# Attention probabilities split before they are turned, and turned by one DMA transpose a tile

## The chip, the cores and the metric

One core of a Trainium2 chip runs the whole program. The metric is device time in microseconds (us) of one execution. The engines are PE (TensorE: matmuls, and transposes by a matmul with the identity), DVE (VectorE), ACT (ScalarE), POOL (GpSimd) and SP (SyncE, which here only issues DMAs). Each takes its instructions in the order in which the program lists them; semaphores make one wait for another.

## What is computed

Two layers on 4 x 256 tokens of width 256. The change lies in the first block, a cross attention over 256 + 1601 = 1857 keys in each of 4 batches, with 16 query heads that share 4 key heads. Cut to what matters:

```
kv_in = concat(context, x)                     # 1857 rows
k = rope(rms_norm(kv_in @ Wk));  v = kv_in @ Wv          # 4 heads of 128
q = rope(rms_norm(x @ Wq))                               # 16 heads of 128
probs = softmax(q k^T * SCALE);  attn = probs v;  x = x + attn @ Wo
```

Behind it come a mixture of experts, a window attention and a feed-forward block, which the change leaves as they are.

## The kernel before

Values of full precision are kept as two bf16 halves, a high part and the rest (low part), and a product is three bf16 matmuls: high x high, high x low, low x high. A **group** is one batch and one key head: its keys K, its values V, and 8 query **tiles** of 128 queries (4 heads x 2 halves of the 256 tokens). There are 16 groups, so 128 tiles. The code unrolls groups 0 and 1, a loop of two groups a turn (even `u = 0`, odd `u = 1`), and groups 14 and 15.

A group has 8 **slots**, one for each tile. In a slot PE forms the scores of tile t (`form_scores`, 12 matmuls in 4 PSUM banks of up to 512 keys), DVE takes the maximum of each bank (`row_max`), and ACT the exponential into `prob`, in f32 (`exponent`). One slot later the probabilities are turned, since the value product needs keys on the partitions: `turn_probs` turns 15 blocks of 128 x 128 on PE into the PSUM buffers `pT_ps`, ACT copies the high half into `pT` (`probs_high`), DVE subtracts it from PSUM for the low half (`probs_low`), and `apply_values` makes 45 matmuls from `pT` and V. These steps go in four quarters j.

The rest of a slot is work of the group's neighbours, from the table `SLOTS`, in three places (ahead of, amid and behind the value products): for the next group the projections `KV` 0 to 7 and `Q` 0 and 1 and the small turns `KT` and `QT`; for this group or the one before (`-`) the turned output `AT` and the output projection `WO`. All use the PSUM buffer `aux`. POOL computes norm and rope of every projected row (`rope`), in `POOL_ORDER`; DVE the sums of squares and the low half of V (`raw_rows`).

SP's whole program in this stage is a loop over the groups of

```
sp.wait_ge(s["kp_done"], nth("KV", PAIRS - 1, n - 2))
sp.wait_ge(s["qp_done"], nth("Q", 1, n - 2))
...                                   # DMAs of wkv, kvT, wq, tab
sp.wait_ge(s["wo_done"], nth("WO", 1, n - 2))
...                                   # DMA of wo
```

so that the loads of group n + 1 follow the wait for `WO` 1 of group n - 2, which stands in slot 1 of group n - 1.

Of the kernel before, what the change touches and what calls it, by code (L numbers as in the profile page):

```python
# [6 lines left out]
BF16 = mybir.dt.bfloat16  # L7
# [3 lines left out]
ALU = mybir.AluOpType  # L11
# [4 lines left out]
P = 128  # L16
# [10 lines left out]
NB = len(BANKS)  # L27
PAIRS = (KT + 1) // 2
# [66 lines left out]
def prepare(nc, t, x):  # L95
# [295 lines left out]
SLOTS = [  # L391
    ([], [("KV", 0)], [("KV", 1)]),
    ([("AT-", 1)], [("KV", 2)], [("WO-", 1)]),
    ([], [("Q", 0)], [("KV", 3)]),
    ([], [("Q", 1)], [("KV", 4)]),
    ([("KT", 0)], [("KV", 5)], [("KV", 6)]),
    ([("AT", 0)], [("KV", 7)], [("QT", 0)]),
    ([("KT", 1)], [("WO", 0)], [("QT", 1)]),
    ([("KT", 2)], [("KT", 3)], []),
]  # L400
FIRST_GROUP = [("KV", 0), ("KV", 1), ("KV", 2), ("Q", 0), ("KV", 3), ("Q", 1), ("KV", 4), ("KV", 5), ("KV", 6),
               ("KV", 7), ("QT", 0), ("QT", 1), ("KT", 0), ("KT", 1), ("KT", 2), ("KT", 3)]
POOL_ORDER = [x for x in FIRST_GROUP if x[0] in ("KV", "Q")]
# [26 lines left out]
def attend(nc, t, x, groups=GROUPS):  # L430
# [4 lines left out]
    with Scope(nc, "att") as sc:  # L435
# [22 lines left out]
        mx = sc.sb("mx", [P, 2, NB])  # L458
        negmax = sc.sb("negmax", [P, 4])
        es = sc.sb("es", [P, 4, NB])  # L460
        rsum, rinv = sc.sb("rsum", [P, 4]), sc.sb("rinv", [P, 4])
        prob = sc.sb("prob", [P, 2, KP])
# [4 lines left out]
        windows = sc.sb("windows", [P, 2, WIN * ROW])  # L467

        scores = sc.ps("scores", [P, NB * 512])
        pT_ps = [sc.ps(f"pT{i}", [P, 4, P]) for i in range(2)]  # L470
        out_ps = sc.ps("out", [P, 2, HD])
        aux = sc.ps("aux", [P, 512])
# [4 lines left out]
                 "exp_done", "pt_done", "pt_hi", "pt_lo", "pv_done", "sum_ready", "rinv_ready", "o_done", "seg_in", "row_ready"]  # L477
# [3 lines left out]
        gathered, stored = ([sc.sem(f"{n}{i}") for i in range(2)] for n in ("gathered", "stored"))  # L481
        DONE = {"KV": "kv_done", "Q": "q_done", "KT": "kt_done", "QT": "qt_done", "AT": "at_done", "WO": "wo_done"}
# [25 lines left out]
        with nc.Block() as block:  # L508
            @block.sync
            def _(sp):  # L510
                def load_group(n, par, b, h):
                    if not isinstance(n, int) or n >= 2:

                        sp.wait_ge(s["kp_done"], nth("KV", PAIRS - 1, n - 2))
                        sp.wait_ge(s["qp_done"], nth("Q", 1, n - 2))
# [5 lines left out]
                    if isinstance(n, int) and n == 0:  # L521
                        for dst, src in ((kw, "kw_l"), (qw, "qw_l"), (ident, "ident_l")):
                            sp.dma_start(dst[:, :], t[src]).then_inc(s["const"], 16)
                        sp.dma_start(segt_i[:, :], t["segt_l"]).then_inc(s["seg_in"], 16)
# [4 lines left out]
                load_group(0, 0, 0, 0)  # L529
                load_group(1, 1, 0, 1)  # L530
                if groups > 2:
                    with sp.Fori(1, groups // 2) as p:
                        for u in range(2):
                            load_group(2 * p + u, u, p // 2, 2 * (p % 2) + u)

            @block.tensor
            def _(pe):
                before = []

                def task(kind, n, ahead, g, u):  # L540
                    gt = g + ahead
                    par = (u + ahead) % 2
                    if before:
                        bk, bn, bg = before.pop()
                        wait(pe, s[FREE[bk]], nth(bk, bn, bg))
                    before.append((kind, n, gt))
                    if kind == "KV":
# [38 lines left out]
                def form_scores(g, u, i):  # L586
# [3 lines left out]
                    for k, (lo, n) in enumerate(BANKS):  # L590
                        if i == 0:
                            pe.wait_ge(s["kt_lo"], nth("KT", k, g))
                        wait(pe, s["exp_done"], NB * (tile - 1) + k + 1)
# [5 lines left out]
                def turn_probs(tile, i, j):  # L599
                    wait(pe, s["exp_done"], NB * tile + j + 1)  # L600
                    wait(pe, s["pt_lo"], NB * tile + j - 1)
                    for m in range(quad(j)):
                        k0 = (4 * j + m) * P
                        last = nc.tensor.transpose(pT_ps[j % 2][:, m, :], prob[:, i % 2, k0:k0 + P], ident[:, :])  # L604
                    last.then_inc(s["pt_done"], 1)

                def apply_values(tile, i, j, g, par):
                    if i == 0 and j == 0:
                        pe.wait_ge(s["v_lo"], nth("KV", PAIRS - 1, g))
                    if j == 0:  # L610
                        wait(pe, s["o_done"], tile)
                    pe.wait_ge(s["pt_lo"], NB * tile + j + 1)
                    for m in range(quad(j)):
                        k = 4 * j + m
                        for a, w in ((0, 0), (0, 1), (1, 0)):
                            last = nc.tensor.matmul(out_ps[:, i % 2, :], pT[:, i % 2, a, k, :], V[:, par, k, w, :],  # L616
                                                    start=(k, a, w) == (0, 0, 0), stop=(k, a) == (KT - 1, 1))
# [3 lines left out]
                def slot(i, g, u, first, prep, last):  # L621
                    ahead, amid, behind = (tasks_of(place, prep, first, last) for place in SLOTS[i])
                    old = not (first and i == 0) and not (last and i > 0)
                    tile, oi = TILES * g + i - 1, (i - 1) % TILES
                    og, opar = (g, u) if i else (g - 1, 1 - u)
                    if old:
                        turn_probs(tile, oi, 0)
                        turn_probs(tile, oi, 1)
# [4 lines left out]
                    if old:  # L633
                        apply_values(tile, oi, 0, og, opar)
                        turn_probs(tile, oi, 2)
                        apply_values(tile, oi, 1, og, opar)
                        turn_probs(tile, oi, 3)
# [8 lines left out]
                def group(g, u, first, prep):  # L646
                    if before:

                        bk, bn, _ = before.pop()
# [1323 lines left out]
```

## Time and profile before

| | |
|---|---|
| median of 3 runs | 2138.71 us (2136.34 to 2139.88) |
| profiled execution: its own time, its span | 2130.99 us, 2129.2 us |
| attention, groups 0 to 15 | some 184 to 1376 us of the span |
| PE busy | 1805.2 us (85%) |
| DVE, ACT, POOL busy | 1453.1, 1074.8, 1080.8 us |

The profile is one execution. Times are counted from the start of its span. Matmuls are pipelined, so the time between the starts of two rows says more of PE than their durations.

### The profile page before, as it was taken

To read this page: it belongs to the slowest core of one execution; us is meant where nothing else is said; L and a number is where in the kernel's file an instruction comes from. 1 tells how busy PE (TensorE), PEld (TensorE's weight loads), DVE (VectorE), ACT (ScalarE), POOL (GpSimd) and SP (SyncE) were. 2 spreads that over 40 slices of the span, in tenths; PEclk is the share of its full clock that TensorE was granted. 3 is DMA by queue.
4 is the path that set the end of the run, shared out by engine and by line. 5 is a ranking of instruction groups with operands and counts; after the bars stand their busy time and mean duration, and the time that the engine had idled before them with its cause. 6 is when DMAs were issued, how large, how long until landed. Compare 5 with 4: busy or idle time off the path is not lost. (4 is left out here: it accounts for less than half of the span.)

```text
span 2129.2 us, 44379 instructions
## 1 busy us (share of the span) xinstructions
PE 1805.2 (85%) x14711; PEld 1352.4 (64%) x14711; DVE 1453.1 (68%) x3940; ACT 1074.8 (50%) x2650; POOL 1080.8 (51%) x1641
## 2 busy tenths in 40 slices
PE   3447999999999999999999999757888887378997
PEld 3425788777777877877877787543544444136884
DVE  7746887877778778778868877646445554456656
ACT  2414766666666666766767766520222222054443
POOL 4413786676667659657756865100345544154110
PEclk8657999999999999999999999956989998676998
DMA  6671022112202202201220203332367766420100
GB/s 264 245 306 71 2 82 82 35 50 82 82 3 82 82 3 82 82 28 57 82 83 2 82 12 101 108 140 81 108 192 215 212 203 180 139 56 9 41 15 24
DMA packets 74760, 202.58 MB, mean 95 GB/s; under 512 B 9945, under 2 KB 40770, under 8 KB 71170
## 3 DMA queue, kind: packets, MB, share of 16 engines
q1 hardware_dynamic: 61346, 163.70, 22.8%
q0 software_dynamic: 9984, 30.42, 4.4%
q10 hardware_dynamic: 3168, 5.24, 0.7%
q8 instruction: 131, 2.15, 0.4%
q14 instruction: 131, 1.07, 0.2%
HBM read 161.67 MB, written 37.66 MB: 94 GB/s over the span
## 5 line engine op out<-in xcount | busy, mean ns | idle before, releaser
L857 DVE TENSOR_TENSOR att_pT<-att_pT 128x512 bf16<-128x512 f32 (+1 forms) x512 | 321.9, 651 | 198.4 <-ACT att_pT L754 195.7
L616 PE MATMUL att_out<-att_V,att_pT 128*128 128x128 bf16 x5760 | 385.9, 219 | 10.0 <-DVE att_pT L857 8.3
L754 ACT ACTIVATE att_pT<-att_pT 128x512 bf16<-128x512 f32 (+1 forms) x512 | 278.3, 572 | 201.4 <-PE att_pT L604 201.4
L616 PEld LDWEIGHTS att_out<-att_V,att_pT 128*128 128x128 bf16 x5760 | 350.2, 98 | 36.7 <-DVE att_pT L857 19.6
L760 ACT ACTIVATE att_prob<-att_scores,att_negmax 128x512 f32<-128x512 f32 (+1 forms) x512 | 329.5, 653 | 15.8 <-DVE att_negmax L846 14.6
L595 PE MATMUL att_scores<-att_K,att_Q 128*128 128x512 bf16 (+1 forms) x1536 | 331.0, 366 | 0.0
L844 DVE TENSOR_REDUCE att_mx<-att_scores 128x1 f32<-128x512 f32 (+1 forms) x512 | 292.2, 631 | 4.6 <-PE att_scores L595 4.5
L604 PE MATMUL att_pT<-att_ident,att_prob 128*128 128x128 f32 x1920 | 278.2, 276 | 17.4 <-issue 17.4
L595 PEld LDWEIGHTS att_scores<-att_K,att_Q 128*128 128x128 bf16 x1536 | 153.0, 100 | 149.0 <-issue 11.0
L555 PE MATMUL att_aux<-att_wkv,att_kvT 128*128 128x256 bf16 x1440 | 188.1, 282 | 42.4 <-DMA att_kvT<-kv_s 21.1
L604 PEld LDWEIGHTS att_pT<-att_ident,att_prob 128*128 128x128 f32 x1920 | 211.5, 142 | 19.1 <-issue 18.2
L555 PEld LDWEIGHTS att_aux<-att_wkv,att_kvT 128*128 128x128 bf16 x1440 | 139.6, 101 | 69.8 <-DMA att_kvT<-kv_s 21.3
L695 POOL TENSOR_TENSOR att_scaled<-att_kvraw,att_kw 128x256 f32<-128x256 f32 x120 | 82.9, 691 | 192.8 <-ACT att_kvraw L735 192.8
L1235 POOL DMA_INDIRECT y_s<-moe_ysb,moe_result_row x80 | 79.2, 990 | 156.8 <-ACT moe_ysb L1343 155.5
L697 POOL TENSOR_TENSOR att_cosd<-att_scaled,att_tab 128x256 f32<-128x256 f32 (+2 forms) x150 | 123.4, 823 | 11.8
L1333 ACT ACTIVATE moe_silu<-moe_up 128x176 f32<-128x176 f32 x96 | 30.4, 317 | 183.8 <-PE moe_up L1291 137.0
L1230 POOL DMA_INDIRECT moe_xg<-xrow_s,moe_token_row x80 | 77.6, 970 | 86.8 <-DVE moe_token_row L1400 62.2
L1291 PE MATMUL moe_up<-moe_wa,moe_xT 128*128 128x352 f32 x320 | 121.1, 506 | 0.0
L709 POOL TENSOR_TENSOR att_rs<-att_rs,att_nhalf 128x2 f32<-128x2 f32 (+2 forms) x150 | 119.4, 796 | 0.0
L735 ACT ACTIVATE att_kvraw<-att_aux 128x512 f32<-128x512 f32 (+1 forms) x128 | 73.1, 571 | 83.9 <-PE att_aux L555 83.3
L1418 DVE COPY moe_hT<-moe_ht 128x256 f32<-128x256 f32 x96 | 40.6, 423 | 100.3 <-PE moe_ht L1298 100.1
L760 ACT ACTIVATION_READ_ACCUMULATOR att_prob<-att_scores,att_negmax 128x1 f32 x512 | 108.8, 212 | 0.0
(299 smaller groups left out, 3286.2 us busy)
## 6 DMA issues: line engine op xcount, KB each, us to landing
moe_wa<-in_wa_l SPq DMA_DIRECT2D x80, 480.0 KB
att_kvT<-kv_s SPq DMA_DIRECT2D x16, 1920.0 KB
att_tab<-tab_s SPq DMA_DIRECT2D x16, 960.0 KB
att_wq<-wq_s SPq DMA_DIRECT2D x16, 512.0 KB
att_wo<-wo_s SPq DMA_DIRECT2D x16, 512.0 KB
kv_s<-prep_kvhl SPq DMA_DIRECT2D x4, 1920.0 KB
prep_kv<-in_ctx_l SPq DMA_DIRECT2D x4, 1664.0 KB, 7.6
moe_y<-y_s SPq DMA_DIRECT2D x8, 768.0 KB, 4.6
```

What stands on the lines that cost most here:

```text
L555: last = nc.tensor.matmul(o, kvT[:, par, a, c, k0:k0 + P], wkv[:, par, w, c, :], start=(c, a, w) == (0, 0, 0), stop=(c, a) == (DC - 1, 1))
L595: last = nc.tensor.matmul(scores[:, lo:lo + n], Q[:, u, a, i, :], K[:, u, w, lo:lo + n], start=(a, w) == (0, 0), stop=a == 1)
L604: last = nc.tensor.transpose(pT_ps[j % 2][:, m, :], prob[:, i % 2, k0:k0 + P], ident[:, :])
L616: last = nc.tensor.matmul(out_ps[:, i % 2, :], pT[:, i % 2, a, k, :], V[:, par, k, w, :], start=(k, a, w) == (0, 0, 0), stop=(k, a) == (KT ...
L695: eng.tensor_tensor(a, raw[:, 0:m, :], weight[:, :].unsqueeze(1).to_broadcast([P, m, HD]), ALU.mult).then_inc(linked, 1)
L697: eng.tensor_tensor(b.rearrange("p m (e f) -> p m e f", e=2), a.rearrange("p m (e f) -> p m e f", e=2), cos.unsqueeze(2).to_broadcast([P, ...
L709: eng.tensor_tensor(scale, scale, nhalf[:, 0:m], ALU.pow).then_inc(linked, 1)
L754: nc.scalar.activation(pT[:, i % 2, 0, 4 * j:4 * j + m, :], pT_ps[j % 2][:, 0:m, :], ACT.Copy).then_inc(s["pt_hi"], 1)
L760: nc.scalar.activation(prob[:, i % 2, lo:lo + n], scores[:, lo:lo + n], ACT.Exp, bias=negmax[:, i % 4:i % 4 + 1], scale=1.0, accum_out=es[ ...
L844: nc.vector.reduce_max(mx[:, i % 2, k:k + 1], scores[:, lo:lo + n], AX.X).then_inc(s["bank_max"], 1)
L857: nc.vector.tensor_tensor(pT[:, i % 2, 1, 4 * j:4 * j + m, :], pT_ps[j % 2][:, 0:m, :], pT[:, i % 2, 0, 4 * j:4 * j + m, :], ALU.subtract) ...
L1291: last = nc.tensor.matmul(up_ps[j % 2][:, 0:GU], rows, w[:, c * GU:(c + 1) * GU], start=c == 0, stop=c == DC - 1)
```

## The change

- The probabilities are split while queries are still on the partitions. ACT copies `prob` into the high half of the new tile `phl` (bf16), DVE subtracts it from `prob`; both in two **spans** of up to 1024 keys (`SPANS`), not four banks. The maxima and exponentials go by spans too.
- PE's turns are gone. SP issues one `dma_start_transpose` a tile, of both halves of `phl` (128 x 3840, bf16) into `pT`, when DVE has done the low half. This is one slot after the scores.
- The value products follow two slots behind the scores, the scaled output three.
- The PSUM banks set free become a second buffer for the tasks (`aux0`, `aux1`) and one bank for each output.
- `SLOTS` is written anew: `Q` 0 and 1 in slot 0, then `KV` 0 to 7, and POOL works in that order.
- SP's program is now written in slots, with the loads between the transposes.
- `windows`, used at the end of the stage, is laid over `tab`.

The diff, cut to its core:

```diff
 SLOTS = [
-    ([], [("KV", 0)], [("KV", 1)]),
...
+    ([], [("Q", 0)], [("Q", 1)]),
+    ([], [("KV", 0)], [("KV", 1)]),
...
+                def turn(tile, i):
+                    sp.wait_ge(s["p_lo"], NS * (tile + 1))
+                    sp.sem_inc(s["turning"], 1)
+                    sp.dma_start_transpose(pT[:, i % 2, :, :, :].rearrange("p a k q -> p (a k) q"),
+                                           phl[:, i % 2, :, :].rearrange("p a k -> p (a k)")).then_inc(turned[i % 2], 16)
+
+                def slot(i, g, u, first, prep, last):
+                    if not (first and i == 0) and not (last and i > 0):
+                        turn(TILES * g + i - 1, (i - 1) % TILES)
+                    if i == 0 and prep and not first:
+                        load_first(*batch_head(g, u, 1))
+                    if i == 4 and prep and not first:
+                        n, par, _, h = batch_head(g, u, 1)
+                        load_wo(n, par, h)
...
                 def apply_values(tile, i, j, g, par):
-                    pe.wait_ge(s["pt_lo"], NB * tile + j + 1)
+                        wait(pe, s["o_done"], tile - 1)
+                        pe.wait_ge(turned[i % 2], 16 * (TILES // 2 * g + i // 2 + 1))
...
+                def probs_high(tile, i, g, k):
+                    lo, n = SPANS[k]
+                    act.wait_ge(s["exp_done"], NS * tile + k + 1)
+                    if k == 0:
+                        wait(act, turned[i % 2], 16 * (TILES // 2 * g + i // 2))
+                    nc.scalar.activation(phl[:, i % 2, 0, lo:lo + n], prob[:, i % 2, lo:lo + n], ACT.Copy).then_inc(s["p_hi"], 1)
...
+                def probs_low(tile, i, g, k):
+                    lo, n = SPANS[k]
+                    dve.wait_ge(s["p_hi"], NS * tile + k + 1)
...
+                    nc.vector.tensor_tensor(phl[:, i % 2, 1, lo:lo + n], prob[:, i % 2, lo:lo + n], phl[:, i % 2, 0, lo:lo + n],
+                                            ALU.subtract).then_inc(s["p_lo"], 1)
```

`load_first` holds the waits for `kp_done` and `qp_done` and the DMAs of wkv, kvT, wq and tab; `load_wo` the wait for `wo_done` and the DMA of wo; `batch_head(g, u, 1)` names the group after g.

**PE, slot 0 of group 1** (a slot with the first tasks for group 2). L595/L625 are the scores, L604 the turns, L616/L638 the value products, L555 a `KV` projection, L592 a `Q` projection. Before:

```order
L604 MATMUL att_pT<-att_ident,att_prob 128x128 x8
L595 MATMUL att_scores<-att_K,att_Q 128x512 x9
L595 MATMUL att_scores<-att_K,att_Q 128x321 x3
L616 MATMUL att_out<-att_V,att_pT 128x128 x12
L604 MATMUL att_pT<-att_ident,att_prob 128x128 x4
L616 MATMUL att_out<-att_V,att_pT 128x128 x12
L604 MATMUL att_pT<-att_ident,att_prob 128x128 x3
L555 MATMUL att_aux<-att_wkv,att_kvT 128x256 x12
L616 MATMUL att_out<-att_V,att_pT 128x128 x21
L555 MATMUL att_aux<-att_wkv,att_kvT 128x256 x12
```

Now, up to the scores of slot 1:

```order
L625 MATMUL att_scores<-att_K,att_Q 128x512 x9
L625 MATMUL att_scores<-att_K,att_Q 128x321 x3
L638 MATMUL att_out<-att_V,att_pT 128x128 x24
L592 MATMUL att_aux<-att_wq,att_kvT 128x512 x6
L638 MATMUL att_out<-att_V,att_pT 128x128 x21
L592 MATMUL att_aux<-att_wq,att_kvT 128x512 x6
L625 MATMUL att_scores<-att_K,att_Q 128x512 x9
```

The turns are gone, and the first task that reads the next group's wq and kvT is a `Q` in the middle of slot 0.

**SP, group 1 and the last of group 0.** The eight transposes are those of slots 1 to 7 of group 0 and of slot 0 of group 1. Before, after the loads at the start of the stage, SP's loop over the groups began at once, with nothing between the loads:

```order
L518 DMA att_wkv<-wkv_s 128x1024
L518 ISA
L518 DMA att_kvT<-kv_s 128x7680
L519 ISA
L519 DMA att_wq<-wq_s 128x2048
L520 ISA
L520 DMA att_tab<-tab_s 128x1920
L527 DMA att_wo<-wo_s 128x2048
```

Now:

```order
L541 DMA_TRANSPOSE att_pT<-att_phl 128x30x128 x8
L522 DMA att_wkv<-wkv_s 128x1024
L522 DMA att_kvT<-kv_s 128x7680
L523 DMA att_wq<-wq_s 128x2048
L524 DMA att_tab<-tab_s 128x1920
L541 DMA_TRANSPOSE att_pT<-att_phl 128x30x128 x4
L529 DMA att_wo<-wo_s 128x2048
L541 DMA_TRANSPOSE att_pT<-att_phl 128x30x128 x3
```

The loads for group 2 stand behind the transpose of slot 0 of group 1, in the same queue.

## Rows read from the trace of the kernel before

**Rows 1.** The page: busy time (share of the span) x instructions.

```profile
PE 1805.2 (85%) x14711; PEld 1352.4 (64%) x14711; DVE 1453.1 (68%) x3940; ACT 1074.8 (50%) x2650; POOL 1080.8 (51%) x1641
```

**Rows 2.** By stretch: length, PE, PEld, DVE, ACT, POOL, clock, DMA, GB/s.

```profile
230.00:1400.00 1170.00, 1103.91 (x11209) 892.02 (x11206) 899.43 (x2311) 772.50 (x1989) 753.90 (x1320) 0.98 0.18 65
```

**Rows 3.** Waits from 400 to 1300 us: total us, times, longest.

```profile
PE att_out L616 <- DVE att_pT L857: 3.4, 11, 0.3
```

**Rows 4.** PE in order of time, one slot and the next scores: start, us.

```profile
201.42 2.52 PE L595 MATMUL att_scores<-att_K,att_Q 128*128 128x512 bf16 x12
203.77 0.83 PE L616 MATMUL att_out<-att_V,att_pT 128*128 128x128 bf16 x12
204.44 0.61 PE L604 MATMUL att_pT<-att_ident,att_prob 128*128 128x128 f32 x4
...
207.18 1.34 PE L616 MATMUL att_out<-att_V,att_pT 128*128 128x128 bf16 x21
208.36 1.47 PE L555 MATMUL att_aux<-att_wkv,att_kvT 128*128 128x256 bf16 x12
209.67 1.04 PE L604 MATMUL att_pT<-att_ident,att_prob 128*128 128x128 f32 x8
210.54 2.52 PE L595 MATMUL att_scores<-att_K,att_Q 128*128 128x512 bf16 x12
```

**Rows 5.** SP's queue in order of time, two rounds of loads.

```profile
346.10 0.33 SPq L527 DMA_DIRECT2D att_wo<-wo_s  x1
347.18 0.33 SPq L518 DMA_DIRECT2D att_wkv<-wkv_s  x1
...
419.18 0.33 SPq L527 DMA_DIRECT2D att_wo<-wo_s  x1
```

**Rows 6.** By stretch, while a group's loads run; the last number is GB/s.

```profile
348.00:354.00 6.00, 6.00 (x69) 4.70 (x67) 5.57 (x15) 3.68 (x11) 5.84 (x13) 1.00 0.95 329
354.00:358.00 4.00, 4.00 (x30) 2.79 (x29) 1.69 (x4) 2.73 (x8) 3.76 (x7) 1.00 1.00 417
```

**Rows 7.** DMA issues: KB each, median us from issue to landing.

```profile
all_x<-in_x_l SPq DMA_DIRECT2D x1, 1024.0 KB, 5.1
...
out<-all_x SPq DMA_DIRECT2D x8, 128.0 KB, 1.7
```

**Rows 8.** SP's DMA queue: packets, MB, share of 16 engines' span.

```profile
q1 hardware_dynamic: 61346, 163.70, 22.8%
```

**Rows 9.** Order in time, one slot: scores, maxima, the first low half after.

```profile
704.53 2.52 PE L595 MATMUL att_scores<-att_K,att_Q 128*128 128x512 bf16 x12
...
706.40 2.28 DVE L844 TENSOR_REDUCE att_mx<-att_scores 128x1 f32<-128x512 f32 x4
...
709.10 0.69 DVE L857 TENSOR_TENSOR att_pT<-att_pT 128x512 bf16<-128x512 f32 x1
```

**Rows 10.** DVE by shape: busy us, mean ns; last row from 500 us on.

```profile
L342 DVE TENSOR_TENSOR prep_kvhl<-prep_kv,prep_kvhl 128x1920 bf16<-128x1920 f32 x4 | 19.9, 4965 | 2.3 <-ACT prep_kvhl L253 2.3
...
L697 DVE TENSOR_TENSOR att_cosd<-att_scaled,att_tab 128x256 f32<-128x256 f32 x7 | 3.0, 425 | 0.2
...
L695 DVE TENSOR_TENSOR att_scaled<-att_qraw,att_qw 128x512 f32<-128x512 f32 x2 | 1.4, 689 | 0.0
...
L832 DVE TENSOR_TENSOR att_V<-att_kvraw,att_V 128x256 bf16<-128x256 f32 x54 | 31.7, 588 | 0.0
```

**Rows 11.** PE in order of time, around the loop's end.

```profile
476.47 1.97 PE L604 MATMUL att_pT<-att_ident,att_prob 128*128 128x128 f32 x8 [3.48 <-issue]
478.23 4.53 PE L595 MATMUL att_scores<-att_K,att_Q 128*128 128x512 bf16 x12
```

**Rows 12.** PE in order of time, scores of two slots of group 15.

```profile
1303.70 2.52 PE L595 MATMUL att_scores<-att_K,att_Q 128*128 128x512 bf16 x12
...
1311.31 2.52 PE L595 MATMUL att_scores<-att_K,att_Q 128*128 128x512 bf16 x12
```

**Rows 13.** PE in order of time, one of five small turns of the first group.

```profile
178.05 1.12 PE L567 MATMUL att_aux<-att_ident,att_kp 128*128 128x128 f32 x4 [1.41 <-DVE att_K L819]
```

More of the change, by code:

```diff
@@ L27 @@
 NB = len(BANKS)
+SPANS = [(k, min(1024, NK - k)) for k in range(0, NK, 1024)]
+NS = len(SPANS)
 PAIRS = (KT + 1) // 2
@@ L622, in slot @@
                     ahead, amid, behind = (tasks_of(place, prep, first, last) for place in SLOTS[i])
[L623 to L628, printed above, removed]
+                    old = not (first and i < 2) and not (last and i > 1)
+                    tile, oi = TILES * g + i - 2, (i - 2) % TILES
+                    og, opar = (g, u) if i >= 2 else (g - 1, 1 - u)
                     if not last:
@@ L654, in tail @@
                 def tail(g):
[L655 to L657 removed]
+                    before[:] = [(bk, bn, g - 1) for bk, bn, _ in before]
+                    for i in range(TAIL):
                         slot(i, g, 0, False, False, True)
@@ L770, in slot @@
                     tile, oi = TILES * g + i, (i - 1) % TILES
-                    old = not (first and i == 0) and not (last and i > 0)
-                    if old:
-                        probs_high(tile - 1, oi, 0)
-                        probs_high(tile - 1, oi, 1)
-                    if not (first and i < 2) and not (last and i > 1):
-                        output(tile - 2, (i - 2) % TILES)
+                    if not (first and i < 3) and not (last and i > 2):
+                        output(tile - 3, (i - 3) % TILES)
+                    if not (first and i == 0) and not (last and i > 0):
+                        for k in range(NS):
+                            probs_high(tile - 1, oi, g if i else g - 1, k)
                     for kind, n in projected(i, prep):
@@ L862, in slot @@
                     tile, oi = TILES * g + i, (i - 1) % TILES
-                    old = not (first and i == 0) and not (last and i > 0)
-                    if old:
-                        probs_low(tile - 1, oi, 0)
-                        probs_low(tile - 1, oi, 1)
                     if not last:
@@ L870, in slot @@
                         task(*x_, g, u)
-                    if old:
+                    if not (first and i == 0) and not (last and i > 0):
                         row_sum(tile - 1, oi)
-                        probs_low(tile - 1, oi, 2)
-                        probs_low(tile - 1, oi, 3)
+                        for k in range(NS):
+                            probs_low(tile - 1, oi, g if i else g - 1, k)
                     for kind, n in projected(i, prep):
```

151 lines of the change are left out of this document (69 added, 82 removed).

## Prediction

> **What bounds the kernel now.** I read the page first: PE is busy for 85% of the span [rows 1]. The table by stage then shows where: from 230 to 1400 us, the attention, PE is busy for 1103.91 of 1170 us at a granted clock of 0.98, DVE for 899.43 [rows 2]. The list of waits from 400 to 1300 us shows no long wait of PE: for the low halves of the probabilities it waits 3.4 us in all [rows 3]. So the attention is PE's own work, end to end. The order in time of one slot gives its parts, start to start: scores 203.77 - 201.42 = 2.35 us; value products 0.67 us for 12, so 0.67 + 0.67 + 1.18 = 2.5 us for 45; turns 0.87 us for 8, so 1.65 us for 15 [rows 4]. SP issues the loads of a group once in 419.18 - 346.10 = 73.1 us [rows 5]: eight slots of 9.14 us. What is left for projections and small turns is 9.14 - 2.35 - 2.5 - 1.65 = 2.6 us a slot.
>
> **What it removes.** The 15 turns on PE: 9.14 - 1.65 = 7.5 us of PE work a slot. If nothing else moved, 15 groups x 8 x 1.65 = 198 us, and some 13 us in the last group, were gained. DVE has 899.43 / 128 = 7.0 us of work a slot (the window holds all 128 tiles but a few) [rows 2], so it could follow.
>
> **What it adds: one DMA transpose a tile.** It moves 2 x 1920 x 128 x 2 bytes = 983 KB from SBUF to SBUF. The trace has no such operation. From below: the plain loads of a group run at 329 GB/s over 6 us and at 417 over the next 4, 364 in the mean [rows 6]; at 365 GB/s it is 2.7 us, and a small transfer (128 KB) lands after 1.7 us [rows 7]. That gives L = 4.4 us from issue to landing; a plain load of 1024 KB landed in 5.1 us [rows 7], in line with it. From above: the destination is written in rows of 256 bytes, 3840 of them, 240 for each of 16 engines. SP's queue moved 61346 packets in 22.8% of 16 engines' span, 0.127 us a packet [rows 8]; if each row cost a mean packet, L = 30 us. I take L = 6.5 us, near the lower end, since in bytes and engines it is most like the plain load, with half as much again for the short rows.
> The Trainium skill (DMA: Bandwidth & Descriptors, section Latency and other measured facts) gives 261 GB/s for a transpose DMA in one kernel. With that, an estimate, L = 3.8 + 1.7 = 5.5 us, and the sum below would come to 2330 us. No row here shows a transpose, so the sum goes by the bounds.
>
> **The chain that L lies on.** Call the start of a slot's scores S. Scores end at S + 2.35; the second of the two maxima takes 833 columns after that, about 0.95 us (2.28 us for 1857 columns in four pieces [rows 9]); maximum, sum and reciprocal bring the first low half to S + 3.8 (before it began 4.57 us after the scores at 704.53, after four reductions that ended late [rows 9]). The low halves are two subtractions, 1857 columns, now with both operands in SBUF. From below: in the first group, where POOL does little, two operands in SBUF cost DVE 0.425 us for 256 columns and 0.689 for 512, so 1.03 ns a column and 2.1 us for the two. From above: beside POOL's long subtractions of the preparation 1920 columns took 4.965 us, so 4.8 us. Between: the value rows' subtraction of 256 columns takes 0.588 us in the attention, 1.4 times 0.425; so 2.9 us [rows 10]. The tile is ready to turn at S + 6.9 with 0.2 us for the hand-over. Its value products stand one slot on, at 2.35 us into it. They start at S + 6.9 + L, and behind them in PE's order stand 2.5 + 2.6 us before the scores two slots after S. Two slots take 12.0 + L, one 6.0 + L/2: with L = 6.5, 9.25 us, with L = 4.4, 8.2 us. PE's 7.5 us are not reached unless L is 3 us. DVE and ACT have room in 9.25 us. So the 1.65 us come back as a wait for the transpose.
>
> **The loads move behind the turns, and next to their use.** Before, SP issued the loads for a group's preparation after the output projection in slot 1, and the first projection that reads them stood in slot 0 of the next group, six slots on; two rounds of loads are 73 us apart [rows 5]. Now SP's program is in slots. In slot 0 of a group it first waits for the low halves of the last tile (S + 6.9), issues that transpose, and then wkv, kvT, wq and tab of the next group; and PE's first projection of the next group, Q 0, stands in the middle of that same slot 0, at S + 2.35 + 1.25 = S + 3.6. Nothing hides this: behind Q 0 in PE's order stand the other value products, Q 1 and the scores of tile 1; ACT and DVE run dry, and POOL waits for raw rows. wq is landed after the transpose has left the engines (L - 1.7) and 2.75 MB (256 + 1920 + 512 KB) are through, 7.5 us at 365 GB/s, and 1.7 us more: S + 6.9 + (L - 1.7) + 9.2. Then follow Q 0 (1.3), the other half of the value products (1.25) and Q 1 (1.3). Slot 0 lasts 6.9 + (L - 1.7) + 9.2 + 3.85 = 18.25 + L: 24.75 us, some 17 of them PE standing still. These are 14 loads, in groups 1 to 14.
> After 3.48 us of idle at the loop's end PE ran at half clock: 8 turns took 1.97 us (1.04 before), 12 matmuls of the scores 4.53 us (2.52) [rows 4, 11], 0.93 + 2.01 = 2.9 us in all. I charge 2.9 us once a stall. The loop's end itself stays.
>
> **The group.** From the start of slot 1: its own 7.5 us (no wait, slot 0 was long), then three pairs of slots: 7.5 + 3 x (12.0 + L) = 43.5 + 3L. With slot 0 and the clock: 64.65 + 4L. With L = 6.5: 90.65 us against 73.1, +17.55. Times 14: **+246 us**.
>
> **Small terms.** Groups 0 and 15 have no load to wait for. Group 0: 9.25 instead of 9.14 a slot, +1. In group 15 (slots of 1311.31 - 1303.70 = 7.6 us [rows 12]) POOL is idle: 6.0 + L + 2.5 + 0.6 for two slots, 7.8 us, +2. The first group's small turns get two PSUM buffers instead of one: five waits of about 1.4 us [rows 13] shrink, -5. The last tile gets a transpose in its chain, +4. Fewer, longer instructions on ACT and DVE (8 fewer a tile) lie beside PE: 0. The value buffers, output two slots later, and windows laid over tab cost nothing while POOL's gather ends in group 15. Together +2.
> Sum: 2130.99 (the profiled execution) + 248 = 2379. The median of the runs shown is 7.7 us above the profiled one, so **2387 us**.
>
> **The rivals.**
> *The transpose is slow.* SP's queue works one after the other; with L of 12 us and more it is the bound in every slot. For: the short rows. Against: 16 engines with full rows ran at 417 GB/s [rows 6]. L = 12: 14 x (64.65 + 48 - 73.1) = +554, 2693 us. 0.22.
> *DVE's subtraction is the worse half.* With 4.8 instead of 2.9 us the chain grows by 1.9 in slot 0 and in each pair, 7.6 x 14 = +106: 2492 us. POOL is busy for 753.90 of 1170 us, with short instructions [rows 2], which speaks for less. 0.12.
> *The transpose is as fast as a plain copy.* L = 4.4: 64.65 + 17.6 = 82.25, +128: 2268 us. 0.13. The Trainium skill (Advanced Engine Details and Errata, section X-Bar Transpose) has transposes at the rate of regular DMAs on trn2, which would be this case; no row here can show it.
> *Not slower.* The loads come early enough after all: this decides from the point where they are issued 9.2 us before S + 3.6, so in the slot before. Against it is SP's order: its wait for the low halves of the tile before can't end until DVE has done the maxima of slot 0, which need PE's scores of slot 0. Even a transpose that costs nothing leaves slot 0 at 6.9 + 9.2 + 3.85 = 19.95, and with the clock and 7 slots of 7.5 us 75.35 us a group, +2.25, 31 us in all: with 26 us won in groups 0 and 15 and 5 at the start, 2139 us, no change. Were the loads hidden too, 2139 - 198 - 13 - 5 = 1923 us. Together 0.06.
>
> **How the numbers follow.** Forecast 2387 us, chance 0.47, its own range 2320 to 2450 (L from 5.4 to 7.7). Leaving out most of the slow transposes and of the last rival: 2250 to 2620. What is within 0.2% can't be told from no change. Faster 0.04 (a part of the last rival), same 0.03, slower 0.93.
>
> **What would show it.** In the profile after: PE in slot 0 waits for DMA wq some 15 to 20 us, 14 times; value products wait for the DMA of pT about 1.5 to 2 us a slot; the granted clock falls to a half after each long wait; L of the transposes is 5 to 8 us; subtractions from prob take about 1.5 us each. What would make it wrong: L far from 6.5 us (4 x 14 = 56 us for each us), transposes and loads that share the engines otherwise than one after the other, or a clock that stays low through the slots.

## The result, and the profile after

| | before | after |
|---|---|---|
| median | 2139.3 us (4 runs) | 2480.31 us (4 runs, 2473.93 to 2529.39) |
| profiled execution: own time, span | 2130.99, 2129.2 us | 2478.94, 2477.1 us |
| ratio | | 1.1553, 95% interval 1.1441 to 1.1666 (a disturbed run, 2529.39, left out) |
| a group, first scores to first scores, mean of groups 1 to 14 | 74.9 us | 97.5 us |

The change costs 341 us. From the page of after, the busy times, and SP's DMA queue:

```profile
PE 1679.5 (68%) x12661; PEld 1207.2 (49%) x12791; DVE 1466.4 (59%) x3428; ACT 990.8 (40%) x1882; POOL 1229.3 (50%) x1641
...
q1 hardware_dynamic: 556962, 289.54, 47.2%
```

PE's busy time fell by 126 us and its share by 17 points [rows 1] (130 of its matmul records are missing: PEld has 12791). POOL, whose instructions are the same 1641 as before, is busy 148 us longer; I come back to that. By stretch, after, with columns as in [rows 2]:

```profile
230.00:1400.00 1170.00, 781.54 (x7259) 589.69 (x7353) 717.76 (x1435) 544.93 (x984) 730.41 (x1075) 0.85 0.55 125
```

No engine is busy for more than 67% of the stage: it is bound by waits. These are PE's largest, 500 to 1300 us (eight groups; total us, times, longest). Before, its wait for the turned low halves was 3.4 us from 400 to 1300 us [rows 3]:

```profile
PE att_aux L592 <- DMA att_wq<-wq_s: 124.8, 8, 17.0
...
PE att_out L638 <- DMA att_pT<-att_phl: 87.3, 41, 4.3
...
PE att_scores L625 <- issue: 24.8, 5, 6.8
```

Slot 0 of a group and the next slots on PE, in order of time, as in [rows 4]:

```profile
541.22 3.58 PE L625 MATMUL att_scores<-att_K,att_Q 128*128 128x512 bf16 x11 [6.83 <-issue]
...
544.64 1.50 PE L638 MATMUL att_out<-att_V,att_pT 128*128 128x128 bf16 x24
...
563.13 2.74 PE L592 MATMUL att_aux<-att_wq,att_kvT 128*128 128x512 bf16 x6 [16.98 <-DMA att_wq<-wq_s]
565.66 2.31 PE L638 MATMUL att_out<-att_V,att_pT 128*128 128x128 bf16 x21
...
569.11 2.52 PE L625 MATMUL att_scores<-att_K,att_Q 128*128 128x512 bf16 x12
...
581.97 2.74 PE L638 MATMUL att_out<-att_V,att_pT 128*128 128x128 bf16 x24 [2.86 <-DMA att_pT<-att_phl]
```

SP's queue in slot 0, and below it all transposes (duration on SP, then issue to landing, min/median/max):

```profile
548.71 4.48 SPq L541 DMA_TRANSPOSE att_pT<-att_phl  x1
553.70 0.35 SPq L522 DMA_DIRECT2D att_wkv<-wkv_s  x1
...
554.80 0.33 SPq L523 DMA_DIRECT2D att_wq<-wq_s  x1
```

```profile
L541 SPq DMA_TRANSPOSE att_pT<-att_phl x128: 4399/4504/10693, 190.3 to 1705.4; - x128
...
DMA to landing us min/median/max: 6.3/6.4/12.8
```

Here is the stall: PE is through the first half of the value products at about 546 us and stands still until 563; wkv is issued at 553.70, wq at 554.80.

### The profile page after: what moved, and what is told of

It reads as the page before. It is cut to its first block and busy times, and to the rows that moved or that the text cites. A ratio compares the mean times of both kernels' runs of the same rounds, so it can differ in the third digit from the quotient of the medians.

```text
span 2477.1 us, 38974 instructions
## 1 busy us (share of the span) xinstructions
PE 1679.5 (68%) x12661; PEld 1207.2 (49%) x12791; DVE 1466.4 (59%) x3428; ACT 990.8 (40%) x1882; POOL 1229.3 (50%) x1641
## 5 line engine op out<-in xcount | busy, mean ns | idle before, releaser
L638 PE MATMUL att_out<-att_V,att_pT 128*128 128x128 bf16 x5760 | 422.3, 238 | 205.6 <-DMA att_pT<-att_phl 205.6
L858 DVE TENSOR_REDUCE att_mx<-att_scores 128x1 f32<-128x1024 f32 (+1 forms) x256 | 276.7, 1119 | 466.0 <-PE att_scores L625 466.0
L638 PEld LDWEIGHTS att_out<-att_V,att_pT 128*128 128x128 bf16 x5760 | 392.6, 108 | 248.1 <-issue 121.7
L625 PE MATMUL att_scores<-att_K,att_Q 128*128 128x512 bf16 (+1 forms) x1423 | 315.5, 373 | 37.5 <-issue 32.0
L873 DVE TENSOR_TENSOR att_phl<-att_prob,att_phl 128x1024 bf16<-128x1024 f32 (+1 forms) x256 | 335.4, 1350 | 3.2 <-issue 1.3
L781 ACT ACTIVATE att_prob<-att_scores,att_negmax 128x1024 f32<-128x1024 f32 (+1 forms) x256 | 262.6, 1031 | 157.5 <-DVE att_negmax L860 157.5
L625 PEld LDWEIGHTS att_scores<-att_K,att_Q 128*128 128x128 bf16 x1536 | 154.7, 101 | 191.3 <-issue 54.4
L709 POOL TENSOR_TENSOR att_scaled<-att_qraw,att_qw 128x512 f32<-128x512 f32 x30 | 39.0, 1299 | 410.5 <-ACT att_qraw L756 410.5
L774 ACT ACTIVATE att_phl<-att_prob 128x1024 bf16<-128x1024 f32 (+1 forms) x256 | 236.4, 978 | 0.0
L592 PE MATMUL att_aux<-att_wq,att_kvT 128*128 128x512 bf16 x177 | 64.3, 519 | 240.0 <-DMA att_wq<-wq_s 238.0
L711 POOL TENSOR_TENSOR att_cosd<-att_scaled,att_tab 128x256 f32<-128x256 f32 (+2 forms) x150 | 154.6, 1031 | 11.8
L592 PEld LDWEIGHTS att_aux<-att_wq,att_kvT 128*128 128x128 bf16 x192 | 22.0, 125 | 268.3 <-DMA att_wq<-wq_s 209.6
L842 DVE SCALAR_TENSOR_TENSOR att_kjunk<-att_kvraw 128x128 bf16<-128x128 f32 x240 | 118.8, 527 | 0.0
```

Source lines behind the costliest of these rows:

```text
L625: last = nc.tensor.matmul(scores[:, lo:lo + n], Q[:, u, a, i, :], K[:, u, w, lo:lo + n], start=(a, w) == (0, 0), stop=a == 1)
L638: last = nc.tensor.matmul(out_ps[i % 2][:, 0:HD], pT[:, i % 2, a, k, :], V[:, par, k, w, :], start=(k, a, w) == (0, 0, 0), stop=(k, a) == ...
L709: eng.tensor_tensor(a, raw[:, 0:m, :], weight[:, :].unsqueeze(1).to_broadcast([P, m, HD]), ALU.mult).then_inc(linked, 1)
L711: eng.tensor_tensor(b.rearrange("p m (e f) -> p m e f", e=2), a.rearrange("p m (e f) -> p m e f", e=2), cos.unsqueeze(2).to_broadcast([P, ...
L774: nc.scalar.activation(phl[:, i % 2, 0, lo:lo + n], prob[:, i % 2, lo:lo + n], ACT.Copy).then_inc(s["p_hi"], 1)
L781: nc.scalar.activation(prob[:, i % 2, lo:lo + n], scores[:, lo:lo + n], ACT.Exp, bias=negmax[:, i % 4:i % 4 + 1], scale=1.0, accum_out=es[ ...
```

## The experiments

Each kernel differs from after (or the one named) by the edit shown. In the same series of runs as an experiment the kernel before took 2122.82 to 2135.74 us; ratios are to it.

**Loads early.** SP loads two groups ahead, in slot 0, so a group's data is there a group before its use.

```diff
-                    if i == 0 and prep and not first:
-                        load_first(*batch_head(g, u, 1))
+                    if i == 0 and not last and not (isinstance(g, int) and g + 2 >= groups):
+                        load_first(*batch_head(g, u, 2))
```

> The changed kernel, but the loads of wkv, kvT, wq and tab for group g + 2 are issued in slot 0 of group g (before: for group g + 1, so next to their use). Theory (a wait of 17 us for wq and 2.9 us at half clock in each of 14 groups; the rest of the loss is the transpose in the chain): slot 0 falls to about 10 us, a group from 97.8 to about 83 us, the kernel to 2300 us (2250 to 2350); the wait of PE for wq is gone, the wait for pT stays or grows, because the 4.2 MB stand before the next transpose. Rival (the chain of scores, maxima, low halves and transpose is so slow that the wait in slot 0 only covers it): above 2420 us.

Measured 2265.72 us, ratio 1.0655 (1.0618 to 1.0692). The late loads cost 215 us. A group is now 83.2 us. PE's wait for pT grew, as expected, from 205.6 to 280.1 us over the whole span.

**Loads late, in the kernel before.** The other way round: before gets one more wait ahead of its loads.

```diff
                         sp.wait_ge(s["qp_done"], nth("Q", 1, n - 2))
+                        sp.wait_ge(s["pt_lo"], NB * (TILES * (n - 1) - 1) + NB)
```

> The kernel before with one wait more: SP issues the loads for group g + 1 only when the last low half of group g - 1 is done, which is in slot 0 of group g, where their first projection stands. No other part of the change. Theory: kvT is waited for in the middle of slot 0, some 10 us, and 2.9 us at half clock behind it, 14 times: +185 us, 2325 us (2290 to 2360). Rival (the loads are through before PE comes to them): 2139 us.

Measured 2301.72 us, ratio 1.0826 (1.0783 to 1.0868), 86.8 us a group. The loads alone, placed where the change puts them, make the old kernel slower. PE's wait, 500 to 1300 us:

```profile
PE att_aux L556 <- DMA att_kvT<-kv_s: 87.5, 9, 10.1
```

**No transposes, with late and with early loads.**

```diff
-                    sp.dma_start_transpose(pT[:, i % 2, :, :, :].rearrange("p a k q -> p (a k) q"),
-                                           phl[:, i % 2, :, :].rearrange("p a k -> p (a k)")).then_inc(turned[i % 2], 16)
...
-                        pe.wait_ge(turned[i % 2], 16 * (TILES // 2 * g + i // 2 + 1))
```

> The changed kernel without its transposes: pT is set to zero once at the start, SP still waits for the low halves before it issues the loads, and the value products read zeros (that part of the computation is left out). Theory: no wait for pT; slots 1 to 7 go at 7.7 us, the wait for wq shrinks by the 4.5 us of one transpose to 12 or 13 us; a group takes 78 us and the kernel about 2220 us (2180 to 2260). Rival (DVE and POOL, which share SBUF, hold the slots up and not the transpose): slots of 9 us and more, above 2330 us.

> Both of the edits before: no transposes (zeros in pT) and loads two groups ahead. Theory: what PE's own work gives, 7.6 us a slot, 61 us a group and the loop's ends; 1985 us (1940 to 2030). Rival (DVE or POOL is the bound behind the transposes): 8.5 us a slot or more, above 2080 us.

Measured 2345.33 us, ratio 1.1026 (1.0983 to 1.107), and 2147.25 us, ratio 1.0105 (1.0082 to 1.0127). Both times the rival's number came. The transposes cost 135 us with late loads and 118 with early ones, far from the 260 and 281 that the theory gives (2480 - 2220 and 2266 - 1985); and a kernel with no turns on PE, no transposes and no load to wait for is no faster than before, 76.8 us a group against 74.9. (What follows the last scores takes 765 us here and 771 before, so the other data behind it hardly count.) So a third cost hides behind the first two. In this trace, with transposes gone and loads early, the stage and three of its waits, 500 to 1300 us:

```profile
230.00:1400.00 1170.00, 941.84 (x9356) 706.16 (x9353) 883.37 (x1807) 679.88 (x1243) 906.44 (x1324) 0.93 0.17 60
```

```profile
DVE att_K L829 <- ACT att_K L757: 88.7, 23, 6.7
...
PE att_aux L603 <- DVE att_Q L829: 61.6, 10, 6.5
...
ACT att_kvraw L751 <- POOL att_kp L731: 40.6, 10, 4.1
```

POOL is busy for 906 of 1170 us, against 754 [rows 2]. The order in time beside one pair of DVE's subtractions shows why:

```profile
761.38 0.45 POOL L712 TENSOR_TENSOR att_sind<-att_scaled,att_tab 128x128 f32<-128x128 f32 x1
...
761.82 2.44 DVE L867 TENSOR_TENSOR att_phl<-att_prob,att_phl 128x1024 bf16<-128x1024 f32 x2
761.94 1.44 POOL L718 TENSOR_TENSOR att_cosd<-att_cosd,att_sind 128x128 f32<-128x128 f32 x1
763.34 1.49 POOL L721 TENSOR_TENSOR att_rs<-att_rs,att_nhalf 128x2 f32<-128x2 f32 x1
...
768.52 0.46 POOL L718 TENSOR_TENSOR att_cosd<-att_cosd,att_sind 128x128 f32<-128x128 f32 x1
768.93 0.71 POOL L721 TENSOR_TENSOR att_rs<-att_rs,att_nhalf 128x2 f32<-128x2 f32 x1
```

The same two steps take 1.44 and 1.49 us beside the subtraction and 0.46 and 0.71 without it: 1.8 us more in this slot. Over the stage it is some 1.3 us a slot (906 - 754 us in 122 slots). POOL falls behind, ACT's next copy of raw rows waits for POOL's key, and what stands behind that copy in ACT's, DVE's and PE's orders waits too. That was an argument until the next two runs.

**A maximum in the subtraction's place** (from the kernel without transposes and with early loads).

```diff
-                    nc.vector.tensor_tensor(phl[:, i % 2, 1, lo:lo + n], prob[:, i % 2, lo:lo + n], phl[:, i % 2, 0, lo:lo + n],
-                                            ALU.subtract).then_inc(s["p_lo"], 1)
+                    nc.vector.tensor_reduce(spare[:, i % 2, k:k + 1], prob[:, i % 2, lo:lo + n], AX.X, ALU.max).then_inc(s["p_lo"], 1)
```

> The kernel of the changed program without transposes and with early loads (2147.25 us), in which DVE, in place of subtracting the high half from the probabilities (two operands read from SBUF, one written there), takes a maximum over them (one operand, nothing but one column written). It leaves out the turned probabilities and the low halves. Theory: the subtraction keeps POOL off the SBUF while it runs, POOL's steps take 906 us of the window 230 to 1400 instead of 754, and POOL's late keys hold up ACT, DVE and PE in turn. Then POOL's steps fall back to about 0.5 us for 128x128, POOL has 10 us a group less to do, and the time is 1995, within 1950 to 2050. Rival: it is the length of DVE's own work, or the order of the waits, whatever POOL does: the maxima take about as long as the subtractions (1.1 to 1.35 us each), and the time stays within 2110 to 2160.

Measured 2003.45 us, ratio 0.9333 (0.9238 to 0.9429): 144 us less, 67.2 us a group. POOL's steps in groups, 500 to 1300 us, with the maxima and, below, with the subtractions:

```profile
L719 POOL TENSOR_TENSOR att_cosd<-att_cosd,att_sind 128x128 f32<-128x128 f32 (+2 forms) x103 | 53.7, 522 | 0.0
L712 POOL TENSOR_TENSOR att_sind<-att_scaled,att_tab 128x128 f32<-128x128 f32 (+1 forms) x102 | 52.2, 512 | 0.0
```

```profile
L711 POOL TENSOR_TENSOR att_sind<-att_scaled,att_tab 128x128 f32<-128x128 f32 (+2 forms) x103 | 80.4, 781 | 0.0
L718 POOL TENSOR_TENSOR att_cosd<-att_cosd,att_sind 128x128 f32<-128x128 f32 (+1 forms) x104 | 73.5, 707 | 0.0
```

**The same, with DVE as long as before.** One more maximum over 400 columns a slot.

> As the kernel with maxima in place of the subtraction (2003.45 us), with one more maximum over 400 columns a slot, so that DVE is busy there for as long as the subtractions took (2.7 us a slot, not 2.2). The same parts are left out. It tells the two things apart that the maximum changed at once. Theory, POOL held off the SBUF: DVE's own length costs little, and the time is 2015, within 2000 to 2045. Rival, DVE's length: 0.45 us a slot of DVE gave the gain, and the time goes most of the way back, above 2090.

Measured 2013.54 us, ratio 0.9472 (0.9419 to 0.9524). DVE's length gives 10 us back, or 30 by the ratios (1.3 us a group), not 144. Most of what the subtraction costs is its hold on POOL, not its own time.

**Half a transpose** (from loads early).

```diff
-                    sp.dma_start_transpose(pT[:, i % 2, :, :, :].rearrange("p a k q -> p (a k) q"),
-                                           phl[:, i % 2, :, :].rearrange("p a k -> p (a k)")).then_inc(turned[i % 2], 16)
+                    sp.dma_start_transpose(pT[:, i % 2, 0, :, :], phl[:, i % 2, 0, :]).then_inc(turned[i % 2], 16)
```

> The changed kernel with early loads (2265.72 us), in which the transpose takes the high half alone, so half the bytes; the low half in the turned tile is a constant zero, which leaves the low halves out of the value products' values but not their matmuls. The transpose should occupy SP 2.2 us and land after some 4.2 us instead of 4.4 and 6.4. Theory, a chain of score, split, transpose and value product in each pair of slots with POOL's work beside it: removing the transposes gave 118 us for 6.4 us each, so 2.2 us give 40, and the time is 2225, within 2200 to 2245. Rival A, the working of the prediction (every pair of slots is 12.0 us and the transpose): 2.2 us less in 4 pairs of 15 groups gives 132, 2135. Rival B, the transpose's fixed part is what counts: within 2255 to 2275.

Measured 2172.84 us, ratio 1.0147 (1.0053 to 1.0241): 93 us less, between the theory's 40 and rival A's 132, and neither's number. The transposes:

```profile
L541 SPq DMA_TRANSPOSE att_pT<-att_phl x128: 1306/1596/8371, 193.7 to 1398.3; - x128
...
DMA to landing us min/median/max: 4.1/4.1/11.3
```

Half the bytes land 2.3 us sooner, so the rate is 492 KB / 2.3 us = 214 GB/s, and 1.8 us are fixed. A group takes 77.0 us, as with no transposes at all (76.8): both theories took the cost as a straight line, and it has a knee. At 6.4 us the chain of the pair sets the slots; at 4.1 us something else sets the group. That it is POOL is argued from the equal length alone: the long slots lie elsewhere in the group than without transposes, and PE still waits 140.2 us for pT. The rest of the 118 us lies in the last group (51.2 us from its first to its last scores against 37.7) and behind it.

**The split in its own slot, loads together and spread** (from loads early). ACT's and DVE's steps for tile t move from slot t + 1 to slot t, and the transpose with them; value products stay at t + 2. SP now also waits for the value products of tile t - 2 before it issues the transpose of tile t. In the second kernel the loads go out in slots 0 to 3, kvT in two halves.

```diff
                         exponent(tile, i, 1)
+                        for k in range(NS):
+                            probs_high(tile, i, g, k)
```

> The changed kernel with early loads (2265.72 us), in which ACT makes the high half and DVE the low half in the slot of their own scores, behind the exponentials, and SP issues the transpose there; the value products stay two slots behind. Theory: the chain in a pair of slots is gone, since a transpose now has a whole slot more; what is left is POOL's work and the chain of keys, as without transposes (2147 us), plus what the transposes take of the memory ports: 2165, within 2140 to 2200. Rival: the split in its own slot makes DVE wait for ACT's exponentials and high half within the slot, with the maxima of the next scores queued behind; each slot is then 9 to 11 us, and the time is above 2230.

> As the kernel before it (the split in its own slot), and the loads of a group, which SP issued together in slot 0, are spread over slots 0 to 3. Theory: the five loads in one slot hold back the transpose behind them in slot 1, which then costs some 5 us a group; spread, they cost nothing, and the time is 60 us lower than that of the kernel before it. Rival: the transpose has a slot to spare, so that the loads cost nothing either way: within 10 us of it.

Measured 2277.91 us, ratio 1.0655 (1.0579 to 1.0731), and 2213.27 us, ratio 1.0344 (1.026 to 1.0428). The theory of the first failed: 2165 was expected. The rival's number came, but not by its mechanism, slots of 9 to 11 us: slots 1, 2 and 4 of a group take 6.6 to 7.5 us, slot 3 takes 16 to 19, slots 6 and 7 11 to 16. The second kernel says what a large part of it was: the loads in one slot delay the transposes behind them, and spreading them gives 65 us (60 expected), with 9.3 to 9.8 us for slot 3. PE waits for pT 49.4 us over the whole span then, against 135.9 in the first kernel and 280.1 with loads early.

**Exponentials left in PSUM** (from the last one). A version that computes everything, and frees POOL: DVE's subtraction reads one operand from PSUM. ACT makes the high half of a span right behind its exponential.

```diff
-                        wait(pe, s["exp_done"], NS * (tile - 1) + k // 2 + 1)
+                        wait(pe, s["p_lo"], NS * (tile - 1) + k // 2 + 1)
...
-                    nc.scalar.activation(prob[:, i % 2, lo:lo + n], scores[:, lo:lo + n], ACT.Exp, bias=negmax[:, i % 4:i % 4 + 1],
+                    nc.scalar.activation(scores[:, lo:lo + n], scores[:, lo:lo + n], ACT.Exp, bias=negmax[:, i % 4:i % 4 + 1],
...
-                    nc.vector.tensor_tensor(phl[:, i % 2, 1, lo:lo + n], prob[:, i % 2, lo:lo + n], phl[:, i % 2, 0, lo:lo + n],
+                    nc.vector.tensor_tensor(phl[:, i % 2, 1, lo:lo + n], scores[:, lo:lo + n], phl[:, i % 2, 0, lo:lo + n],
```

> A version that computes all of the output. The split in its own slot and the spread loads (2213.27 us), and ACT writes the exponentials over the scores in PSUM, so that DVE's subtraction reads one operand from PSUM and one from SBUF, as before the change. PE's scores of the next tile then wait for the low half of the same span. Theory: POOL's steps are back at 0.5 us, as with the maxima; a slot is DVE's chain of two maxima, an exponential, a high half and two subtractions, with the second exponential beside it, 7.6 to 8.5 us, and a group 66 to 70 us against 74.9 before the change: 2050, within 2000 to 2120. Rival A: the banks held until the low half put the slot at 9.5 us or more: above 2180. Rival B: it is the transposes' traffic on the memory that slows POOL and DVE, not the subtraction: POOL's steps stay at 0.6 to 0.8 us, and the time above 2150.

Measured 2225.2 us, ratio 1.0478 (1.0407 to 1.0548). The theory was right on POOL and wrong on the time. POOL's steps are back:

```profile
L734 POOL TENSOR_TENSOR att_cosd<-att_cosd,att_sind 128x128 f32<-128x128 f32 (+1 forms) x100 | 51.3, 513 | 0.0
```

It is rival A's number, with slots of 8.7 to 9.0 us in the even stretch (slots 1 to 5) rather than 9.5, and 12 to 16 in slots 6 and 7. The banks are held longer than they need be: DVE's sum of the exponentials stands ahead of the subtractions and waits for the second exponential, and the low half and the next scores wait behind it:

```profile
DVE att_rsum L876 <- ACT att_scores L795: 144.5, 70, 3.4
PEld att_scores L639 <- DVE att_phl L885: 82.9, 50, 2.3
PE att_scores L639 <- DVE att_phl L885: 76.6, 50, 2.5
```

**The sum behind the subtractions, and a levelled table** (each from the one before).

```diff
-                        row_sum(tile, i)
                         for k in range(NS):
                             probs_low(tile, i, g, k)
+                        row_sum(tile, i)
```

```diff
-    ([], [("KV", 3)], [("KV", 4)]),
-    ([], [("WO-", 1)], [("KV", 5)]),
-    ([], [("KV", 6)], [("KV", 7), ("KT", 0)]),
-    ([], [("QT", 0), ("KT", 1)], [("AT", 0), ("QT", 1)]),
+    ([], [("KV", 3)], [("WO-", 1), ("QT", 0)]),
+    ([], [("KV", 4)], [("QT", 1), ("KT", 0)]),
+    ([], [("KV", 5)], [("KV", 6)]),
+    ([], [("KT", 1)], [("KV", 7), ("AT", 0)]),
```

> The kernel with exponentials in PSUM (2225.2 us), with DVE's sum of the exponentials behind its two subtractions instead of ahead of them. All of the output is computed. There DVE waits 2 us a slot for both exponentials (144.5 us in the window 500 to 1300) before the first subtraction, which ACT's high half would have let it start 1.3 us earlier. Theory, the low half of the first span sets the next scores and so the slot: 1 to 1.3 us a slot in most slots, 2080, within 2040 to 2130. Rival: the second span ends last (DVE's second subtraction waits for ACT's second high half), the bank of the third quarter of the scores comes free as late as before, and the time stays above 2195.

> As the kernel before it, and the table of tasks is levelled: QT 0 in slot 3, QT 1 and KT 0 in slot 4, one task fewer in slot 5, KT 1, KV 7 and AT 0 in slot 6, where slots 5 and 6 held three and four. Theory: slots 6 and 7 of a group take 12 us each, since PE's third and fourth task wait for aux, which ACT and DVE empty at the end of their slot (PE waits for DVE att_Q and att_K 8 us a group); with three at most, and their inputs long ready, 5 to 6 us a group go: 75 us below the kernel before it, within 40 to 110. Rival: any third task waits as long, and three slots have one now as before: within 25 us of it.

Measured 2151.03 us, ratio 1.0105 (1.0037 to 1.0172), and 2158.3 us, ratio 1.0141 (1.0078 to 1.0204). The moved sum gives 74 us, half of what was expected; slots 1 to 4 are 7.6 to 8.2 us, but slots 6 and 7, with four and three tasks, still 11 to 13, and slot 7 16 at the loop's end. The levelled table gives nothing, which is its rival's number: slots 5 and 6 are up to 2 us shorter, slots 3 and 4 1.1 to 1.6 us longer. 2151 us is the best that I found with DMA transposes, 1% above the kernel before.

## Why the prediction was right, and where it was wrong

The forecast was 2387 us, range 2250 to 2620; measured 2480 us, in the range, slower as forecast. Of the two mechanisms that it names, the late loads are the largest cost, and the wait for the transposes is there; but a third cost, which it does not have, is larger than the second. The pieces of the 341 us, each from a pair of runs and in this order of undoing: late loads 215 (2480 - 2266), transposes 118 (2266 - 2147), POOL held up by the subtraction 144 (2147 - 2003), and against them 136 us (2139 - 2003) by which the kernel that is left, without turns and without low halves, is faster than before. In another order the pieces can be others. The kernel before itself lay between 2123 and 2139 us from series to series; measured from it in each series the pieces are 202, 118, 153 and 132, so each holds to about 15 us.

In the same parts the prediction has 233 us for the late loads ((90.65 - 8 x 9.25) x 14), 231 for the transposes (what is left of 2387 - 1923), nothing for POOL and 216 gained. The transposes are 113 us too dear and the loads 18, the gain is 80 too large, and 144 us are missing. These errors partly cancel: it is partly luck that the total is nearer than its parts. The mechanism held where the sum works it out, in the slots with a wait for wq or for a transpose; it did not hold for the kernel without them.

- **L = 6.5 us**: 6.4 measured, 4.6 us for the bytes and 1.8 fixed, where 4.8 and 1.7 were taken. It was neither the plain copy's rate (the rival at 4.4 us) nor a row at the price of a mean packet (30 us): the queue moved 495,616 packets more than [rows 8], 3872 for each transpose and so about one a row, yet each transpose was through in 4.5 us. That 6.5 was hit is luck in part: the "half as much again" for short rows had no row behind it, and each us of L is 56 us of the sum. The Trainium skill (DMA: Bandwidth & Descriptors, Latency and other measured facts) has 261 GB/s for one kernel; this trace has 214. Its statement that transposes run at the rate of regular DMAs (Advanced Engine Details and Errata, X-Bar Transpose) doesn't hold here: [rows 6] has 417 GB/s for plain loads, and the stretch with a transpose alone has 218, its DMA share full:

```profile
551.00:553.00 2.00, 0.00 (x0) 0.00 (x0) 0.00 (x0) 0.00 (x0) 0.00 (x0) 0.50 1.16 218
```

- **Slot 0**: 24.75 us and 2.9 for the clock, 27.65; measured 25.6 to 29.1. PE's wait for wq, said to be 15 to 20 us, was 16.98 in the slot shown and 15.6 in the mean (124.8 in 8). The order was right, the reason for the later issue partly not: it isn't that loads queue on the DMA engines behind the transpose, SP itself is held 4.48 us by it and issues wkv at 553.70. The experiments with loads early and with loads late in the kernel before confirm the step by 215 and 175 us, where the sum has 233.
- **Three pairs of 12.0 + L = 18.5 us**: in group 13 they took 19.7, 18.2 and 21.8 us. The low halves came as said: 2.9 us was taken, between 2.1 and 4.8, and in groups 1 to 14 they took 2.74 in the mean. Alone they took 2.17, beside POOL 3.72:

```profile
546.45 2.17 DVE L873 TENSOR_TENSOR att_phl<-att_prob,att_phl 128x1024 bf16<-128x1024 f32 x2
...
580.70 3.72 DVE L873 TENSOR_TENSOR att_phl<-att_prob,att_phl 128x1024 bf16<-128x1024 f32 x2
```

So they are not what is in the 4.2 us. Two other things are. The clock: it was charged once a group, but it also falls in the pairs. Behind the wait of 2.86 us at 581.97 the granted clock is 0.50, the lower of its two levels (1.2 of 2.4 GHz), and 24 value matmuls take 2.74 us instead of 1.50:

```profile
582.00:583.00 1.00, 1.00 (x10) 1.00 (x11) 1.00 (x2) 0.61 (x2) 1.00 (x1) 0.50 0.03 8
```

In group 13 it fell so twice in the pairs (24 value matmuls took 2.58 and 2.74 us), for some 3 us together with the matmuls behind them, an estimate. And POOL's lateness in the third pair, where PE waits for the key before the next group's scores:

```profile
1519.26 0.52 PE L597 MATMUL att_aux<-att_ident,att_kp 128*128 128x128 f32 x3 [2.88 <-POOL att_kp L733]
```

The wait of the value products, said to be 1.5 to 2 us a slot, was 1.3 (87.3 us, 500 to 1300 us, in 65 slots).
- **The group, +17.55 us**: measured 22.6. Over 14 groups the difference is 71 of the 100 us by which the sum for the profiled execution was short (2379, measured 2479). Some 9 of the 71 are the loop's end, which "stays" in the prediction: its idle time went from 3.48 [rows 11] to 5.0 us in the mean (24.8 us, 5 times, in the waits above), and there are six turns.
- **Group 15, +2**: this small term was the worst of all in proportion. First scores to the last slot's scores took 75.3 us against 54.4, +21. Slots alternate between some 15 and 7 us. With POOL's gathers and moved rows beside them transposes land late, after 10.5 us in the median (6.4 before that) and 12.8 at the most, and the DMA engines are full:

```profile
1616.00:1691.00 75.00, 44.92 (x412) 35.16 (x418) 33.90 (x52) 30.39 (x51) 13.12 (x16) 0.82 0.95 214
```

Eight transposes of 983 KB in 75 us are 105 of these 214 GB/s. PE waits for the transposes up to 8.68 us; below are the scores of one slot and the value products that waited:

```profile
1639.75 2.30 PE L625 MATMUL att_scores<-att_K,att_Q 128*128 128x512 bf16 x11
...
1657.93 4.96 PE L638 MATMUL att_out<-att_V,att_pT 128*128 128x128 bf16 x45 [8.68 <-DMA att_pT<-att_phl]
```

The last tile's chain, from its scores to the last output projection, took 28.8 us against 18.1, +10.7 where +4 was said. Group 0 came as said: its first scores 5.3 us earlier (-5) and 72.2 us against 71.7 (+1).
- **"DVE and ACT have room", and "Were the loads hidden too ... 1923 us"**: here the working was wrong, not only a size. It summed busy time and asked whether an engine has room; it never asked what DVE's new instruction does to POOL, which the prediction names only as a reason for DVE's price. With no transposes and early loads the time is 2147, not 1923. 144 of the 224 us between them are POOL's (the maximum's run and its longer twin); the other 80 were not taken apart by a run. In the maximum's trace slot 6 of a group takes 11.2 to 11.9 us, where PE waits for DVE att_Q, slot 7 takes 8.4 to 9.5, or up to 13.1 at the loop's end, and the others 6.6 to 9.1. The wait in slot 6, 500 to 1180 us:

```profile
PE att_aux L604 <- DVE att_Q L830: 45.9, 11, 4.2
```

At 4.2 us a group it would be 58 of the 80 us, an estimate. The error stayed small in the total because, it seems, the waits for wq and the transposes covered most of POOL's lateness: POOL's steps ran long in after too (it is busy 148 us longer), but it had 97.5 us a group for them.
- The Trainium skill (SBUF — State Buffer, Who interferes with whom) has the rule that the prediction should have weighed: a VectorE instruction with two inputs in SBUF contends with a GpSimd instruction that reads SBUF, and one with at most one such input does not. The runs agree on both halves: 0.46 us becomes 1.44 beside the subtraction from SBUF; with the maximum (one input) and with the subtraction from PSUM the step's mean is 0.52 and 0.51 us.

Three things stay open: why half of the expected gain of the moved sum did not come; what part of the last group's late transposes is POOL's DMA traffic and what the bursts of that stage, which was not tried by itself; and whether POOL or something else sets the group at half a transpose.

## What to carry to other kernels

When work is moved off the bound engine, ask three things of each step that replaces it: on which queue it now stands ahead of something else (a transpose holds SP for 4.5 us, and PE stood 17 us for a load issued behind it and next to its use), how its latency divides over the slots it must fit in, and which memory its operands are in. An operand moved from PSUM to SBUF, with no more columns and no more instructions, cost 144 us here once the loads and the transposes were out of the way, through an engine whose steps the diff only puts in another order. Undo costs one by one: with two gone, the third was larger than the second, and none of them could be read from the sum of the busy times.

## What the runs showed of the hardware

- A DMA transpose of 983 KB, SBUF to SBUF, bf16, took 6.4 us and one of half the size 4.1: a straight line through the two is 1.8 us and 214 GB/s. SP's queue was held for 4.5 of the 6.4 us, and by the half for only 1.6 us. Plain DMAs held it 0.33 us.
- A DVE subtraction with two operands in SBUF stretched POOL's instructions beside it two- to threefold (0.71 to 1.49 us, 0.46 to 1.44), and a pair of such subtractions took 3.72 us beside POOL and 2.17 alone.
- ACT wrote the exponentials over the scores that it read in PSUM; over 1024 columns this took 1.09 us, against 1.11 with the result in SBUF.
